# Six local-attention layers behind one full attention: the 32x32 block transposes of the probabilities move behind the next tile's maxima on VectorE

## The reference

```python
q, k, v = split(shift_tokens(x) @ Wqkv)          # 16 heads of 64
q, k = rotary(l2norm(q) * qs), rotary(l2norm(k) * ks)
sim = q . k * 8, over the query's window of 32 and the one before it, masked
out = softmax(sim) @ v
x = out @ Wo + x
xn = layernorm(shift_tokens(x)); a, gate = split(xn @ W1 + b1)
x = a * gelu(gate) @ W2 + b2 + x
```

## Time and profile before

| | us |
|---|---|
| timed runs: median of 3 | 2282.62 |
| lowest and highest of them | 2280.07, 2282.78 |
| the profiled execution, its own time | 2277.0 |
| its span, first to last instruction | 2275.2 |
| mean granted TensorE clock | 0.974 of full speed |

### The profile page before, as it was taken

How to read it: one execution, slowest core, us unless ns; L and a number is a source line. 1 busy time by engine, 2 the same in 40 slices (tenths; PEclk the granted TensorE clock), 3 DMA queues, 4 the chain that set the end, 5 groups by cost and what they waited for, 6 DMA issues and landing times. The chain is left out here.

```text
span 2275.2 us, 69842 instructions
## 1 busy us (share of the span) xinstructions
PE 2103.4 (92%) x28313; PEld 1287.8 (57%) x28313; DVE 1984.4 (87%) x2379; ACT 1770.7 (78%) x4234; POOL 1311.7 (58%) x1084
## 2 busy tenths in 40 slices
PE   5999999999998689999999999999999999999986
PEld 2122222222221477777777777677777777777764
DVE  7999999999990788989898999888898999899984
ACT  3388888888887577878787888788787878788873
POOL 4201101111100788878787888787787878888870
PEclk8699999999999799999999999999999999999998
DMA  2322222221220233353434334443335333533331
GB/s 43 98 61 77 79 62 90 67 79 47 62 78 8 59 87 75 83 145 84 104 84 126 99 93 104 113 103 86 82 85 141 85 92 85 139 86 98 84 89 52
DMA packets 167798, 194.12 MB, mean 85 GB/s; under 512 B 87414, under 2 KB 107508, under 8 KB 167476
## 3 DMA queue, kind: packets, MB, share of 16 engines
q1 hardware_dynamic: 167220, 189.65, 32.0%
q10 hardware_dynamic: 256, 0.00, 0.0%
HBM read 56.98 MB, written 25.42 MB: 36 GB/s over the span
## 5 line engine op out<-in xcount | busy, mean ns | idle before, releaser
L988 DVE TENSOR_REDUCE mx<-S_ps 128x1 f32<-128x1024 f32 x512 | 601.7, 1219 | 25.5 <-PE S_ps L1288 20.0
L736 ACT ACTIVATE PT<-E_ps 128x512 f32<-128x512 f32 x1024 | 533.4, 603 | 102.3 <-PE E_ps L1297 99.8
L652 POOL TENSOR_TENSOR tc<-tc,ts 128x1024 f32<-128x1024 f32 x192 | 463.1, 2412 | 28.8 <-DVE ts L1050 28.2
L660 POOL TENSOR_TENSOR tc<-tc,rs 128x1024 f32<-128x1024 f32 x192 | 362.7, 1910 | 13.7
L1288 PE MATMUL S_ps<-KS,QS 48*128 48x512 bf16 x1024 | 321.2, 400 | 9.9 <-DVE mx L988 4.7
L805 ACT ACTIVATE pr<-B_ps,mxB 128x64 f32<-128x64 f32 x1536 | 323.8, 371 | 1.6 <-DVE mxB L1069 1.6
L1297 PE MATMUL E_ps<-QS,KS 64*128 64x512 bf16 x1024 | 317.5, 383 | 7.4 <-ACT PT L736 5.2
L594 POOL CAST w_cut_b<-w_raw_b 128x512 fp32r<-128x512 f32 (+1 forms) x48 | 27.6, 574 | 512.5 <-DMA w_raw_b<-in_Wqkv 380.0
L1334 PE MATMUL B_ps<-w_qkv,x_cut 128*128 128x512 f32 x576 | 259.8, 451 | 30.7 <-POOL x_cut L607 8.8
L1305 PE MATMUL O_ps<-PT,va 128*32 128x512 f32 x2048 | 274.1, 607 | 0.0
L1297 PEld LDWEIGHTS E_ps<-QS,KS 64*128 64x128 bf16 x1024 | 79.4, 94 | 338.5 <-ACT PT L736 257.9
(11 more groups left out here) (181 smaller groups left out, 3971.3 us busy)
## 6 DMA issues: line engine op xcount, KB each, us to landing
xy<-pc SPq DMA_DIRECT2D x768, 64.0 KB, 2.0
vs<-v SPq DMA_DIRECT2D x96, 384.0 KB, 3.7
Wqkv_cut<-w_cut_b SPq DMA_DIRECT2D x72, 256.0 KB, 2.4
w_qkv<-Wqkv_cut SPq DMA_DIRECT2D x36, 512.0 KB, 7.3
rot<-in_rot SPq DMA_DIRECT2D x96, 128.0 KB, 2.6
vs<-v SPq DMA_DIRECT2D x96, 128.0 KB, 3.8
w_raw_b<-in_Wqkv SPq DMA_DIRECT2D x36, 256.0 KB, 2.9
W_cut<-w_cut_b SPq DMA_DIRECT2D x24, 170.5 KB, 2.5
```

Source lines behind the costliest of these rows:

```text
L652: e.tensor_tensor(tc[:, :], tc[:, :], m.ts[i][:, :], ALU.add).then_inc(s[f"rot{n}"], 1)
L660: e.tensor_tensor(tc, tc, m.rs[u % 2][2][:, i * H:(i + 1) * H].unsqueeze(2).to_broadcast([P, H, DH]), ALU.mult).then_inc(s[f"{n}_scaled"], 1)
L736: e.activation(m.PT[n % NPT][:, :], turns.bank("probs", n)[:, :], ACT.Exp).then_inc(turns.sem("probs", n), 1)
L988: e.tensor_reduce(m.mx[h % 2][:, i, hf:hf + 1], m.S_ps[n % 2][:, :, :], AX.XY, ALU.max).then_inc(s["sc_max"], 1)
```

## The change

`blocks` is taken out of its place near the end of VectorE's iteration u, where it worked on tile u - 3, and put right behind `maxima(tile(u - 3))`, where it works on tile u - 4. It is the same instruction on the same tile with the same two waits, now in the iteration after, behind the next tile's maxima. No other engine's program changes, and no semaphore count does.

```diff
         if u <= CLOSE:
             ln_root_slope(chunk(u - 7))
         maxima(tile(u - 3))
+        blocks(tile(u - 4))
         rotate_cos(tile(u - 1), 0)
         square_sums(tile(u - 1), 0)
         rotate_sin(tile(u - 1), 0)
@@
         gated(chunk(u - 8), 1)
         deviation(chunk(u - 5))
         add_epsilon(chunk(u - 6))
-        blocks(tile(u - 3))
         if u < CLOSE:
             residual_2(chunk(u - 10))
         first_scale(chunk(u - 6))
```

## The result

The change made the kernel **slower**: 2291.47 us, median of 4 executions (2290.49 to 2295.69), against 2281.35 (2278.58 to 2282.78); ratio 1.005, 95% interval 1.0038 to 1.0062. Six more executions, beside the experiments, gave 1.0089 (1.0072 to 1.0106). The forecast was 2282.7 in a range up to 2290.5, with 0.22 on slower. So the sign is wrong, and the first measurement lies 1 us outside the range. The two intervals don't meet: the same kernel shifted by some 0.4% from one set of runs to another, more than an interval shows. I therefore read differences within a set first, and take none of under 0.4% between sets as shown. One execution of e16 (6486.52 us) and one of e17 (2812.22 us) were in a slow state and are left out of their medians and ratios.

A forecast was written before the change was run, and what follows sets the result against it. TensorE was taken as the bound, the other engines following it. Terms -2.4 - 1.2 + 0.8 + 1.4 + 1.5 = +0.1 us, carried to the median 2282.62, gave 2282.7; own range 2278.5 to 2287, wider 2275.5 to 2290.5.

The forecast's parts named there:

- (a): VectorE work 1.16 us earlier: maxima 0, gated -2.4 us, residual_2 -1.2 us.
- All three waits named: ScalarE's for maxima (1.6 us), TensorE's unnamed ones before the values matmul (2.4), TensorE's for residual_2's bank (3.7).
- (b): VectorE's port: first_scale, now earlier, overlaps GpSimd's rotated in 14 of 23 iterations; taken as 0, bounds 0 and +3.9 us.
- The port's loss: VectorE time lost where first_scale newly overlaps GpSimd's rotated; taken as 0, at most +3.9 us.
- (c): VectorE's wait for scores, no longer filled by blocks: +0.8 us at the first tiles, bounds 0 and +9.3.
- VectorE's losses count: Slower rival: eight late scores and the port's 14 overlaps are not absorbed, +11.1 us, 2293.7; chance 0.06.
- (d): Later blocks delays SyncE's rotation-table load: +1.4 us in 24 chunk iterations; mid-layer taken as 0, bound +5.8.
- rotation tables are late: Slower rival: load_rot becomes GpSimd's regular bound in chunk iterations, +14.1 us, 2296.7, or 2289.7 for half; chance 0.16.
- The other two signs: Signs of a wrong forecast: TensorE's wait for tc or ts grown, or "issue" stalls differing, by more than 5 us.
- (e): The end: the last but one tile's blocks, later, delays the values matmuls to about 2230.1: +1.5 us, bounds 0 and +3.

The follow-up runs named there:

- e16: The kernel before with each rotation table's load issued ahead of the eight moves and nothing else changed: 2272.53 us, ratio 0.9982.
- e17: The kernel before with 41 odd tiles' transposes moved (not the seven ahead of late scores) and the rotation tables' loads ahead of the moves: 2277.28 us, 0.9993.
- e12: The changed kernel with 11 transposes ahead of late scores and tile 94's put back, and the rotation tables' loads ahead of the moves: 2282.35 us, 1.0011.
- e11: The kernel before with only the 11 transposes moved that stand ahead of late scores: 2283.43 us, ratio 1.0024.
- e18: The kernel before with only the transposes of tiles 5, 21, 37 and 69 moved (mid-layer, ahead of gains and rotation table): 2283.43 us, ratio 1.0026.
- e5: The kernel before with only the transposes of the 24 chunk-iteration tiles (4k+2) moved: 2282.96 us, ratio 1.0012.
- e15: The kernel before with only tile 94's transpose, the last but one, moved: 2280.15 us, ratio 1.0006.
- e6: The kernel before with only the transposes of tiles 4k moved, past gated and maxima: 2281.19 us, ratio 1.0020.
- e1: The changed kernel with the transposes of tiles 12, 28, 44, 60 and 76 (ahead of the next layer's weight loads) put back: 2295.74 us, ratio 1.007.
- e13: The changed kernel itself run once more, against the kernel before: 2298.13 us, ratio 1.0089.
- e7: The kernel before with only the odd tiles' transposes moved, past maxima alone: 2289.09 us, ratio 1.0047.
- e2: The kernel before with only the transposes of tiles 12, 28, 44, 60 and 76 (ahead of the next layer's weight loads) moved: 2281.09 us, ratio 1.0005.

## Why the prediction was wrong

**(a) right, and worth nothing that can be seen.** All three waits named went away. Together I had them at -3.6 us. No kernel with the change shows a gain of that size; e12, which has them without the losses named, still stands at 1.0011. I read them as waits that TensorE makes good at its next wait; no run here isolates that.

**(b) right.** The port's loss stayed small. Fourteen first_scales overlap GpSimd's rotated, as forecast: 13 of them for 0.23 to 0.34 us, which makes them about 0.1 us longer (a median of 789 ns instead of 692), 1.4 us in all, and one is blocked for long (2217 ns) instead of two. All 14, and both of the kernel before, end 0.55 us behind the end of rotated. The Trainium skill, "SBUF — State Buffer", section "Who interferes with whom", has a VectorE instruction with two SBUF inputs and a GpSimd instruction that reads SBUF contend for an exclusive lock; these 16 ends agree.

**(c) a term mis-sized: +0.8 us where 5.5 were measured (e11, 2.1 to 8.9).** The bound was right, 8 x 1.16 = 9.3, and so was the mechanism. What failed is the sentence "Soon behind it comes VectorE's wait for the output product, which absorbs it". The rotation stands between: maxima, transpose, then tc and ts, for which TensorE waits itself (7.2 to 12.0 us), before residual_1's wait is reached. I had also counted 8 late scores in one trace and let only the first tiles matter. The rival "VectorE's losses count" named this wait and its condition, at a chance of 0.06. Its 2293.7 is near the 2291.47 by luck: 3.9 of its 11.1 us are the port's, which cost 1.4 us of VectorE at most, and the tables aren't in it.

**(d) the step that failed most: mid-layer taken as 0, where moving its four transposes alone cost 5.9 us (e18, 3.0 to 8.9).** The bound of +5.8 was there, five times 1.16. I argued that at 1365.97 the late table cost nothing, because first_scale was blocked and VectorE was later still. But with the table later still, the rotated that had blocked first_scale begins only at 1371.58, and first_scale is free (0.69 us at 1369.50 in the changed kernel's trace). So VectorE's cover went, and the wait that ended last became GpSimd's tc. A cover read in the old order was used for the new one. The other cover, "elsewhere a stall of TensorE covers it", holds as far as TensorE never waits for tc there; but at tile 23 the stall is longer where the table is late (3.36 us in e18, 2.0 in e17), and at tile 71 it is longer in both. What makes it so isn't shown, and with it stays open how much of the 5.9 us is the table's. The part of (d) that I did price, +1.4 for 24 chunk iterations, was measured at 1.0012 with the end in it (e5, 2.7 us where my terms 1.4 and 1.5 make 2.9). That agreement is luck: rotary waits for rot in no chunk iteration of e5, and for 0.47 us in all in those of the changed kernel. The rival "rotation tables are late" named the right load at 0.16, but put it into the chunk iterations; its sign for them to decide, rotary waiting more than 10 times, never came (7 times). The wait grew in length more than in number. The other two signs stayed just short as well: TensorE's wait for ts grew by 4.8 us of the 5, and the "issue" stalls differ by 1.0.

**(e) about right**: 1.5 forecast, 1.4 by the ratio of e15, whose interval reaches from -1.6 to +4.3. In the trace TensorE's values of tile 94 wait 3.68 us for the moved blocks. Pieces of the chain that ended last in the changed kernel:

```profile
2235.36 1.25 DVE pc L1061
...
2240.97 1.99 DMA xy<-pc
2243.00 3.43 PE B_ps L1397 x64
```

The transpose, the landing of the last of 8 moves, the values: the forecast had the values at about 2230.1, and they start at 2243.00, 12.9 us later, which is what the scores of the tile after it are late by (12.9 us) through all that lies ahead.

**The sum by what was measured**: 5.5 for late scores (e11), 5.9 for the four mid-layer transposes (e18), 1.4 for the end (e15) are 12.8 us or 0.56%, between the 0.50% and 0.89% of the two measurements of the whole. These are 16 of the 96 transposes, and each of the three numbers has 3 us of uncertainty either way; e6, which has only two of the 16, lost 0.20% by itself, so the sum isn't closed. Taking the three away at once leaves 1.0011 (e12).

**What stays open.** e12 stands 0.29% above e16, which has the same loads ahead and no transpose moved; how much of it is a shift between sets isn't told. Their two profiles part most behind tiles 46 (3.9 us, waits for w_qkv), 71 and 92 (2.6 us each, "issue" stalls of 2.69 and 2.38 us). The stall at tile 92, 2.4 to 2.9 us inside the scores, stands in both profiles of the changed kernel, in e1 and in e12, and in no other. The "issue" stalls of 1 to 4 us in every profile recur near every eighth tile (7, 14, 23, 30, 62, 71, 78), with VectorE and the moves' DMAs at work beside them; what they are was not tried. How much of the loss is the clock isn't separated from the stalls ahead of it. The granted clock goes with the time over all executions: 0.9675 on average in the six of e13, 0.9694 in the seven of e7, 0.9726 in e17, against 0.973 in the kernel before.

## What to carry to other kernels

A step moved behind its neighbour costs nothing only if every wait it used to fill, and every queue entry issued behind its result, has cover in the new order; read that cover again after applying the other effects of the same change, for the same move may remove it. Move each group of iterations alone: four well chosen transposes told more here than 96. And look at what stands behind a long row of DMA issues: two lines that put a small, early-ready load ahead of eight moves made the kernel before 0.18% faster (e16, 0.06% to 0.31%, in one set), the only version here that is told from both as faster.

## What was unexpected

- The largest new wait of the changed kernel, 13.2 us for w_qkv, costs nothing that can be seen: alone (e2) it comes with 11.4 us less of "issue" and a ratio of 1.0005 (0.9996 to 1.0015).
- A small load issued right behind others lands late: 4.9 to 6.1 us for the changed kernel's rotation tables behind the six gains' loads, against a median of 2.6.
- Short stalls are often followed by a stretch at half clock (1.2 GHz instead of 2.4). By the trace's clock records the layers' part has 35.7 us of it before and 69.2 after; TensorE's busy time grows by 7.3 us over the span. These are single executions: e16, the fastest kernel, has 55.6 us in its profile. The same stall is followed by half clock in one execution and not in another (the 1.7 us for ts behind tile 39: 12 transposes in 1.50 us before, 2.30 in e2); whether that makes the 12 to 16 us between the executions of one kernel isn't shown.
